# GLA's output projection as three rounded products, with VectorE splitting its input, and GLA's weights loaded in another order

## The reference

```
q, k, v = x @ Wq.T, x @ Wk.T, x @ Wv.T
k_gated = k * sigmoid(x @ Wg.T);  decay = -softplus(x @ Wd.T + bd)
s_t = exp(decay_t) * s_{t-1} + k_t^T v_t;   o_t = q_t s_t
out = o * rsqrt(mean(o*o) + eps) * norm_w * sigmoid(x @ Wog.T)
return out @ Wo.T
```

## Time and profile before

| | us |
|---|---|
| median of 3 runs | 2087.64 |
| the profiled execution, its own time | 2088.27 |
| its span, first to last instruction | 2086.1 |
| PE busy | 1990.2 (95%) |
| DVE busy | 1513.8 (73%) |
| ACT busy | 1288.2 (62%) |
| POOL busy | 599.2 (29%) |
| mean granted PE clock | 0.979 of full |

### The profile page before, as it was taken

One profiled execution on the slowest core, in us unless ns is written; L12 is line 12 of the kernel. 1 busy time (PEld: TensorE's weight loads), 2 busy tenths in 40 slices (PEclk: granted clock), 3 DMA queues, 4 the chain that ended last, 5 costly groups with the idle time before them and its releaser, 6 DMA issues. The chain is left out here.

```text
span 2086.1 us, 42106 instructions
## 1 busy us (share of the span) xinstructions
PE 1990.2 (95%) x16914; PEld 1405.2 (67%) x16914; DVE 1513.8 (73%) x2466; ACT 1288.2 (62%) x2560; POOL 599.2 (29%) x480
## 2 busy tenths in 40 slices
PE   7999999999999998997999999999999999489997
PEld 6743333333333347986888888888888888478996
DVE  7889999999999976895546464646464644468774
ACT  3258888888888876785454545454545454256663
POOL 1200000000000014554334343434343433125554
PEclk9979999999999999999999999999999999789999
DMA  6832232223223222316222122212122212232221
GB/s 231 249 59 66 54 85 61 64 69 70 71 53 84 66 76 67 128 41 173 72 63 92 63 92 63 92 63 92 63 92 63 92 63 82 62 120 77 107 112 71
DMA packets 103490, 180.66 MB, mean 87 GB/s; under 512 B 24232, under 2 KB 65856, under 8 KB 98176
## 3 DMA queue, kind: packets, MB, share of 16 engines
q1 hardware_dynamic: 103296, 177.97, 28.4%
HBM read 138.48 MB, written 38.67 MB: 85 GB/s over the span
## 5 line engine op out<-in xcount | busy, mean ns | idle before, releaser
L741 DVE TENSOR_REDUCE att_sb_mx<-att_ps_psM 128x1 f32<-128x1024 f32 x512 | 624.6, 1221 | 27.6 <-PE att_ps_psM L978 23.8
L1192 ACT ACTIVATE att_sb_pt<-att_ps_psSO 128x512 f32<-128x512 f32 x1024 | 557.1, 597 | 95.2 <-PE att_ps_psSO L996 41.1
L978 PE MATMUL att_ps_psM<-stack_sb_k,stack_sb_q 48*128 48x512 f32 x1024 | 382.3, 454 | 4.6 <-DVE att_sb_mx L741 2.3
L996 PE MATMUL att_ps_psSO<-stack_sb_q,stack_sb_k 50*128 50x512 f32 x1024 | 373.3, 444 | 0.9 <-DMA stack_sb_q<-att_sb_mrow 0.9
L1008 PE MATMUL att_ps_psSO<-att_sb_pt,stack_sb_v 128*32 128x256 f32 x4096 | 326.4, 391 | 8.6 <-ACT att_sb_osb L1185 8.6
L996 PEld LDWEIGHTS att_ps_psSO<-stack_sb_q,stack_sb_k 50*128 50x128 f32 x1024 | 153.2, 185 | 202.8 <-ACT att_sb_pt L1192 155.5
L1008 PEld LDWEIGHTS att_ps_psSO<-att_sb_pt,stack_sb_v 128*32 128x32 f32 x4096 | 82.0, 108 | 192.1 <-issue 102.9
L2310 ACT ACTIVATE glag_sb_sg<-att_ps_psM 128x512 f32<-128x512 f32 x64 | 38.3, 599 | 250.9 <-PE att_ps_psM L2070 250.8
L2535 DVE TENSOR_TENSOR glaj_sb_dm<-att_ps_psSO,glaj_sb_dm 128x512 f32<-128x512 f32 x128 | 82.2, 684 | 133.5 <-PE att_ps_psSO L2190 133.5
L978 PEld LDWEIGHTS att_ps_psM<-stack_sb_k,stack_sb_q 48*128 48x128 f32 x1024 | 156.9, 189 | 19.3 <-DVE att_sb_mx L741 16.4
L2672 POOL TENSOR_TENSOR glaj_sb_dm<-glaj_sb_dm,glaa_sb_masked 128x1024 f32<-128x1024 f32 x64 | 156.5, 2466 | 19.0 <-DMA glaj_sb_dm<-decay_rows 19.0
(11 more groups left out here) (305 smaller groups left out, 4829.0 us busy)
## 6 DMA issues: line engine op xcount, KB each, us to landing
glaj_sb_dm<-decay_rows SPq DMA_DIRECT2D x32, 1024.0 KB, 5.2
qk_parts<-stack_sb_part SPq DMA_DIRECT2D x32, 512.0 KB, 3.3
glai_sb_eg<-decay_exp SPq DMA_DIRECT2D x64, 256.0 KB, 6.3
moe_sb_gb<-gate_rows SPq DMA_DIRECT2D x8, 2048.0 KB, 7.7
stack_sb_q<-qk_parts SPq DMA_DIRECT2D x192, 64.0 KB, 3.0
stack_sb_k<-qk_parts SPq DMA_DIRECT2D x96, 128.0 KB, 4.3
att_sb_rb<-sums SPq DMA_DIRECT2D x32, 256.0 KB
attended<-att_sb_on SPq DMA_DIRECT2D x32, 256.0 KB, 4.9
```

Source lines behind the costliest of these rows:

```text
L741: nc.vector.tensor_reduce(mx[:, qh, 8 * r + c:8 * r + c + 1], psM[:, t % 2, :], AX.X, ALU.max).then_inc(maxima_taken, 1)
L978: mm = pe.matmul(psM[:, t % 2, c * ST:(c + 1) * ST], q[rs, g, qh, j, n * P:(n + 1) * P], k[rs, g, j, c * ST:(c + 1) * ST], start=True, sto ...
L996: pe.matmul(psS[:, ring_slot(pos), :], k[rs, g, j, s * P:(s + 1) * P], q[rs, g, qh, j, :], start=True, stop=True).then_inc(ring_done, 1)
L1192: nc.scalar.activation(pt[:, s % (LAG + 2), ORDER[i], :], psS[:, (pos + 1) % 3, :], ACT.Exp, scale=AD ** -0.5).then_inc(ring_taken, 1)
```

## The change

The output projection of each chunk becomes three f32r products. Its input yT is split on DVE right after the squares' sum: `y_hi` (rounded copy, 128x1024) and `y_lo` (the difference, 128x1024, written over yT). `y_hi` lies over osq. wo is split too, once: `wo_hi` by 8 casts on ACT, `wo_lo` by 8 subtractions on DVE, both in the slot of the first chunk.

Beside it the storage of GLA's weights is exchanged: Wv lies where the queries' storage is free at the end of the FFN's hidden tiles, Wog where Wv was. Wv is loaded a little before Wq, and Wog is loaded right behind Wq instead of after the FFN. The low parts of Wg and Wk are made earlier on DVE. At the start of the FFN, ACT runs a one-column GELU before `copy_outputs`, `shift_xin(2)` stands after the second tile of i = 1 instead of after i = 0, and `add_projected(2)` stands behind `split_hidden(1, 0)`.

```diff
@@ DVE, FFN
             split_hidden(0, 6)
-            add_projected(2)
             for i in range(1, NST):
                 split_hidden(i, 0)
+                if i == 1:
+                    add_projected(2)
...
-                if i in (NST - 2, NST - 1):
-                    gla_low(i - (NST - 2), 0)
+                if i in (NST - 3, NST - 2):
+                    gla_low(0, i - (NST - 3))
+                if i == NST - 1:
+                    gla_low(1, 1)
                 split_hidden(i, 6)
...
                 if i == NST - 2:
                     gla_norm()
-                    gla_low(0, 1)
+                    gla_low(1, 0)
                     gla_low_heads()
-            gla_low(1, 1)
             gla_keys()
@@ ACT, FFN
             over_pairs(act, body)
+            act.wait_ge(f_.const_in, N_CONST)
+            nc.scalar.activation(f_.shift3[:, 0:1], f_.b_h[:, 0:1], ACT.Gelu)
             copy_outputs(2 * NBG - 1, 1)
-            act.wait_ge(f_.const_in, N_CONST)
...
-                if i + 2 < NST:
+                    if i == 1 and f == 1:
+                        shift_xin(2)
+                if 0 < i and i + 2 < NST:
                     shift_xin(i + 2)
@@ storage
-    wv, wv_raw = weight("wv", second_late, second_late)
+    wv, wv_raw = weight("wv", hidden_q, hidden_x)
-    wog, wog_raw = weight("wog", last_q, last_q)
+    wog, wog_raw = weight("wog", second_late, second_late)
+    parts_at = Area(nc, "gla" + "u", residuals.at, residuals.end)
     osq, yT = residuals.sb("osq", [P, J, P]), residuals.sb("yT", [P, J, P])
+    y_hi, y_lo = parts_at.sb("y_hi", [P, J, P], F32R), parts_at.sb("y_lo", [P, J, P], F32R)
@@ SP
         def load_values():
+            sp.wait_ge(f_.h_done, FT * NST)
+            sp.dma_start(wv_raw[:, :, :], ...).then_inc(w_in[2], 16)
             sp.wait_ge(f_.y_done, 2 * (NST - 1))
-            (Wv and Wq)
+            (Wq, then the 8 DMAs of Wog, moved here from load_rest)
@@ PE
         def out_project(c):
-            pe.wait_ge(yT_ready, 2 * c + 2)
+            pe.wait_ge(ylo_ready, c + 1)
             wait_past(pe, y_ready, c)
             if c == 0:
                 pe.wait_ge(const_set, 1)
-                pe.wait_ge(wo_scaled, 2)
+                pe.wait_ge(wo_ready, J)
             for j in range(J):
-                pe.matmul(psW[:, 0:D], yT[:, j, :], wo[:, j, :], start=(j == 0), stop=(j == J - 1))
-            pe.wait_ge(osum_ready, c + 1)
+                pe.matmul(psW[:, 0:D], y_hi[:, j, :], wo_hi[j][:, :], start=(j == 0), stop=False)
+                pe.matmul(psW[:, 0:D], y_lo[:, j, :], wo_hi[j][:, :], start=False, stop=False)
+                pe.matmul(psW[:, 0:D], y_hi[:, j, :], wo_lo[:, j, :], start=False, stop=(j == J - 1))
             pe.matmul(psW[:, D:D + 1], osum[:, :], ones[:, :], start=True, stop=True).then_inc(out_done, 1)
@@ ACT, slot
-                    wait_past(act, osum_ready, c if n or not first(i, 1) else 0)
+                    wait_past(act, out_done, c if n or not first(i, 1) else 0)
                 nc.scalar.activation(osq[...], psO[...], ACT.Square).then_inc(osq_ready, 1)
...
+            if c == 0:
+                high_out()
+        def high_out():
+            act.wait_ge(wo_scaled, 2)
+            for j in range(J):
+                nc.scalar.copy(wo_hi[j][:, :], wo[:, j, :]).then_inc(wo_hi_ready, 1)
...
         def first_values():
+            act.wait_ge(f_.hlo_even, FT // 2 * NST)
+            act.wait_ge(f_.hlo_odd, FT // 2 * NST)
@@ DVE, slot
             take_outputs(1)
             if n == 0 and past:
                 normalize_y(i - 1)
+            dve.wait_ge(osq_ready, 2 * c + 2)
+            nc.vector.tensor_reduce(osum[:, :], osq[:, :, :].rearrange("p j t -> p t j"), AX.X,
+                                    ALU.add).then_inc(osum_ready, 1)
+            dve.wait_ge(osum_ready, c + 1)
+            nc.vector.tensor_copy(y_hi[:, :, :], yT[:, :, :]).then_inc(yhi_ready, 1)
+            dve.wait_ge(yhi_ready, c + 1)
+            nc.vector.tensor_tensor(y_lo[:, :, :], yT[:, :, :], y_hi[:, :, :], ALU.subtract).then_inc(ylo_ready, 1)
+            if c == 0:
+                for j in range(J):
+                    dve.wait_ge(wo_hi_ready, j + 1)
+                    nc.vector.tensor_tensor(wo_lo[:, j, :], wo[:, j, :], wo_hi[j][:, :], ALU.subtract).then_inc(wo_ready, 1)
             if n == 1 and not last:
                 normalize_x(i + 1, 1 - u)
             if n == 2 and not last:
                 decays(i + 1)
-            dve.wait_ge(osq_ready, 2 * c + 2)
-            nc.vector.tensor_reduce(osum[:, :], osq[:, :, :].rearrange("p j t -> p t j"), AX.X,
-                                    ALU.add).then_inc(osum_ready, 1)
```

More of the change, by code:

```diff
@@ L1875, in gla_programs @@
     residuals = area("i", stacks.k_at, 16 * kb)
-    hidden_q, hidden_k, hidden_w = area("j", stacks.q_at, 16 * kb), area("k", stacks.k_at + 16 * kb, 8 * kb), area("l", stacks.part_at, 8 * kb)
+    hidden_q, hidden_k, hidden_w = area("j", stacks.q_at + 8 * kb, 8 * kb), area("k", stacks.k_at + 16 * kb, 8 * kb), area("l", stacks.part_at, 8 * kb)
+    hidden_x = area("s", stacks.q_at, 8 * kb)
     second_late = area("m", pt_at, 32 * kb)
@@ L1901, in gla_programs @@
     rs3 = early_v.sb("rs3", [P, 2, 1])
-    half, ident = f_.half, f_.ident
+    half, half_set, ident = early_v.sb("half", [P, NT]), m.sem("half_set"), f_.ident
     wd_parts, sg = projected_a.sb("wd_parts", [P, 2, KD, P], F32R), projected_b.sb("sg", [P, 2, ST])
@@ L1906, in gla_programs @@
     eg = residuals.sb("eg0", [P, J, P]), residuals.sb("eg1", [P, J, P])
+    parts_at = Area(nc, "gla" + "u", residuals.at, residuals.end)
     osq, yT = residuals.sb("osq", [P, J, P]), residuals.sb("yT", [P, J, P])
-    dm = hidden_q.sb("dm0", [P, GH, P]), hidden_q.sb("dm1", [P, GH, P])
+    y_hi, y_lo = parts_at.sb("y_hi", [P, J, P], F32R), parts_at.sb("y_lo", [P, J, P], F32R)
+    dm = last_q.sb("dm0", [P, GH, P]), last_q.sb("dm1", [P, GH, P])
     kT, qe = hidden_k.sb("kT", [P, J, P]), hidden_k.sb("qe", [P, J, P])
     v = hidden_w.sb("v", [P, 2, HID])
-    wo = last_w.sb("wo", [P, J, D])
+    freed_b, freed_s = area("v", stacks.part_at + 26 * kb, 2 * kb), area("t", beside_at + 16 * kb, 2 * kb)
+    wo_at = Area(nc, "glawo", last_w.at, last_w.end)
+    wo, wo_lo = last_w.sb("wo", [P, J, D]), wo_at.sb("lo", [P, J, D], F32R)
+    wo_hi = [a.sb(f"wo_hi{j}", [P, D], F32R) for j, a in enumerate((
+        projected_c, projected_c, freed_b, freed_b, freed_s, freed_s, early_o, early_v))]
     q, og = last_v.sb("q", [P, J, HALF]), last_v.sb("og", [P, J, HALF])
@@ L1940, in gla_programs @@
     kv_done, decayed, state_ready, state_zero = (m.sem(s) for s in ("kv_done", "decayed", "state_ready", "state_zero"))
+    yhi_ready, ylo_ready, wo_hi_ready, wo_ready = m.sem("yhi_ready"), m.sem("ylo_ready"), m.sem("wo_hi_ready"), m.sem("wo_ready")
     out_done, square_ready, rs3_ready, y_ready = (m.sem(s) for s in ("out_done", "square_ready", "rs3_ready", "y_ready"))
@@ L1981, in load_values @@
         def load_values():
+            sp.wait_ge(f_.h_done, FT * NST)
+            sp.dma_start(wv_raw[:, :, :], wv_t.rearrange("(k p) o -> p k o", p=P)).then_inc(w_in[2], 16)
             sp.wait_ge(f_.y_done, 2 * (NST - 1))
-            for n, d in ((2, wv_t), (3, wq_t)):
-                sp.dma_start(raws[n][:, :, :], d.rearrange("(k p) o -> p k o", p=P)).then_inc(w_in[n], 16)
-        def first_rows():
-            rows_to_dram(0, 0)
-        def load_rest():
-            sp.wait_ge(f_.y_done, 2 * NST)
-            load_decays(0, 0, 0)
+            sp.dma_start(wq_raw[:, :, :], wq_t.rearrange("(k p) o -> p k o", p=P)).then_inc(w_in[3], 16)
             for k in range(KD):
@@ L1999, in load_rest, with first_rows @@
                                      [:, half_p, :, odd]).then_inc(w_in[4], 16)
+        def first_rows():
+            rows_to_dram(0, 0)
+        def load_rest():
+            sp.wait_ge(f_.y_done, 2 * NST)
+            load_decays(0, 0, 0)
             for half_p in range(2):
@@ L2717, in first_root @@
         def first_root():
+            minus_half(nc, pool, half, half_set)
             inverse_root(nc, pool, rs, half, stats, LN, rs_ready)
```

2 lines of the change are left out of this document (1 added, 1 removed).

## The result

| | before | after |
|---|---|---|
| median, us (9 runs each) | 2087.29 | 2082.05 |
| lowest and highest, us | 2086.65, 2089.71 | 2076.8, 2089.27 |
| span of the profiled execution, us | 2086.1 | 2082.2 |
| PE busy in 1000 to 1700, us | 700.00 | 690.58 |

The changed kernel takes 0.9974 of the time before, 95% interval 0.9965 to 0.9984: 0.26% faster, where 0.5% slower was forecast. Its runs scatter over 12.5 us, four times as far as before.

What follows compares the result with a forecast made beforehand. PE, busy throughout 1000 to 1700 us, was taken as the bound. FFN -4.5, transition -5, first chunk +1.4, stretch +12.9, last chunk +5.5 sum to +10.3 on 2088.27; the median forecast is 2098.0 us, range 2090 to 2104.

Steps and rivals of the forecast that it cites:

- the arithmetic of PE: Output projection on PE: 24 f32r matmuls replace eight float32 ones, saving 0.6 us a chunk, 18.6 us over 31 chunks.
- n = 2: Half_supertile slot n = 2: decays move behind the y parts, scores come late, PE loses 1.4 us (last supertile 1.5).
- n = 1 and n = 3: Slots where POOL's work delays y_lo: PE loses 1.05 us at n = 1 (last supertile 2.7), 1.35 at n = 3.
- its cheap case: Slot n = 3: y_hi gets in ahead of POOL's L2680, and PE loses 0.55 us.
- the dear case: Last supertile's n = 1: masks begin sooner, y_hi waits for one and y_lo for the other, PE loses 2.7 us.
- Rival B: y_hi doesn't stand for POOL but takes 1.22 us: -6.2 in all, 2081.5 us; chance 0.20.
- Transition: Entry to GLA: PE's waits of 4.1 us for wk_lo and 6.1 for the queries shrink, -5 us (-3 to -7.6).
- FFN's start: Table load and shift_xin(2) moved, so PE waits less for the first hidden tiles: -4.5 us (-1 to -7).
- first chunk: GLA's first chunk: wo_lo's subtractions behind y_lo delay PE's projection, +1.4 us (0 to +4).
- last chunk: Behind the last osum nothing hides the y parts and PE's clock may halve: +5.5 us (3.8 to 6.7).
- Rival A: DVE wins the port handover from POOL, only n = 2 stalls: -19.6 in all, 2068 us; chance 0.18.
- rival C: Masks get ahead of both y parts in n = 1 and n = 3: +21 at most, half gives 2108; chance 0.12.

Runs made afterwards that it cites:

- Experiment 2: The changed kernel with the decays of n = 2 again ahead of the squares' sum: 2084.76 us, ratio 0.999 to the kernel before.
- experiment 3: The changed kernel with two more POOL operations in each slot n = 3, run beside the decays: 2092.88 us, ratio 1.0022 to the kernel before.
- in 4: The changed kernel with POOL's masks of n = 2 and key weighting of n = 3 waiting for y_lo: 2069.97 us, ratio 0.9913.
- experiment 1: The changed kernel run again without any edit: 2083.35 us, ratio 0.9967 to the kernel before.
- experiment 8: POOL's scaling of wo made to wait for wog_lo: in the changed kernel 2082.56 us, ratio 0.9969; with the projection in float32 2076.03, ratio 0.9935.
- experiment 7: The changed kernel with the three edits at the start of the FFN undone together: 2089.42 us, ratio 1.0002 to the kernel before.
- experiment 10: The changed kernel with three POOL waits (masks, key weighting, wo scaling) and the last chunk by halves: 2066.89 us with take_out moved, 2061.4 in its old place.
- experiment 9: The changed kernel with the last chunk's y_hi and y_lo made by halves, ahead of the squares' sum: 2081.37 us, ratio 0.9958.

## Why the prediction was wrong

The sign was wrong, by 14.1 us between the traces (+10.3 forecast, -3.8 seen). Step by step:

- **What bounds the kernel, and the arithmetic of PE** held: 18.6 forecast, 18.2 seen.
- The stalls of the y parts were priced 18.2 us too dear, the other terms together 4.1 too well. **n = 2 failed, and is 9.9 of the 18.2 us.** With it right the forecast would have been +0.4, no change; the smaller errors in n = 1 and n = 3, 7.6 together, make the rest of the way to faster. The failed step reads "and only then the decays, 4.6 us, to 1482.1". The 4.6 us were read in a place where POOL worked beside them (2.43 us from 1470.00, for which the first scan stood) and carried to one where POOL is idle. The part just ahead of it had shown that 1.4 us of normalizations can stand for 7.59; I used that to price what is added and didn't ask it of what is moved. By the free duration of 3.0, the weighting ends at 1481.7, ahead of PE's 1481.9: no stall. The last supertile has no decays, and its 1.5 us came as 1.4. Experiment 2 shows the duration follow the place, experiment 3 shows the stall follow POOL.
- **n = 1 and n = 3** were right in mechanism (in 4, with POOL made to wait, all of it is gone) and too dear by 4.4 and 3.2 us: in n = 3 y_hi mostly got in ahead of the weighting, which the prediction had as its cheap case, and in the last supertile the dear case came in other executions (experiment 1), not in this one.
- **y_hi** takes 0.69 us free, near the 0.65 taken, and stands for POOL (2.73 in experiment 1). Rival B, whose 2081.5 is nearly the measured time, was right in the number for the wrong reason.
- **Transition:** 2.7 us short. The new wait is the port once more: wog_lo was priced nowhere against the scaling of wo, although the sentence on the scaling names it as late. The 4.1 for wk_lo went whole, and 1.9 for wv_lo came in its place. That the wait for wog_lo is the port is read from the traces and not from a time: it is 1.1 to 8.2 us in the nine traces without experiment 8's wait, and at most 1.3 in the four with it.
- **FFN's start, first chunk, last chunk** were right, the last with its half clock; for the FFN, experiment 7 shows the three edits together.
- **Rival A** (DVE wins the handover) doesn't happen by itself; made to happen by a wait, it gives 2070, where the prediction said 2068.
- Two figures of the prediction don't follow from its own terms, and change nothing: the upper bound of the stretch is +34 and not +31 (12.9, and the 21 of rival C), and A with three quarters of B is 0.33 and not 0.32.
- The Trainium skill's rule of the exclusive lock (SBUF — State Buffer, "Who interferes with whom") is borne out by the scans: two SBUF inputs, 0.39 us alone, 2.01 for the one that began beside POOL and ended 0.28 behind POOL's end. Its sentence "Issue order, not op shape, decides who blocks" is what the scatter looks like here: 0.1 us between y_hi and a mask (experiment 1) decide over 3.4 us of PE's time, wait and clock.

What stays open: the scatter of 12.5 us was not taken apart run by run, as only one execution of each kernel has a trace. That it is the races is argued from the waits that differ between traces, and from the spread, which is 3.3 and 2.2 us in the two kernels of experiment 10, where all of them are ordered; these are spreads of four runs, the 12.5 us of nine. Why five waits of some 2 us were followed by a low clock and three were not is open too. The worth of experiment 8's wait, and of 9 alone, could not be measured.

## What to carry to other kernels

A duration read from a trace belongs to its place: before carrying an instruction with two SBUF inputs, or a copy between SBUF tiles on VectorE, past another, look what GpSimd did beside it there and will do beside it here, and price both. Look at the longest of a group and not at its mean alone: here the mean of 797 ns was one of 2.01 us and three of 0.39. Where VectorE makes something that PE waits for, and GpSimd's work in the same slot has room, let GpSimd wait for it by a semaphore; here two such waits took 11 to 13 us off the changed kernel, whose projection had been worth nothing. A kernel whose runs begin to scatter after a change may have got races for a resource on its critical path; compare PE's waits in two of its traces, as experiment 1 does.

## What the runs showed of the hardware

- A VectorE scan of 112x128 takes 0.39 to 0.43 us with GpSimd idle; one that began 0.70 us into a GpSimd multiplication of 2.43 us took 2.01.
- A VectorE copy of 128x1024 to f32r between SBUF tiles takes 0.69 us with GpSimd idle and 2.73 where it began 0.23 us behind GpSimd's masks; the subtraction of the same size takes 1.23, and 3.30 where it stood between GpSimd's two masks.
- Of the eight waits of 1.9 to 2.4 us at a projection in these traces, five (2.16 in experiment 1) were followed by some 3 us of matmuls 0.21 us apart instead of 0.12 (window clock 0.58), which cost 1.5 us on top of the wait, and three were not (2.30 in experiment 2); behind waits up to 1.4 us it was never seen. Of two waits of 3.4 us one was (clock 0.62, experiment 10) and one was not (1.00, experiment 9). Behind the 5.43 us wait of the last chunk it was 3.9 us at 0.51.
